# A four-layer graph network on one core: the opening's loads, transposes and query projection put in another order

## The reference, cut to what matters

```python
def _gate(h, q, Wg, bg, Wq, bq):        # q: 8 batches x 64 queries x 768
    h3 = h.reshape(B, N, F)
    hg = einsum('bnf,gf->bng', h3, Wg[:, :F])
    qg = einsum('blf,gf->blg', q, Wg[:, F:]) + bg
    attn = sigmoid(hg[:, :, None, :] + qg[:, None, :, :])
    qi = einsum('bnlf,blf->bnf', attn, q)
    alpha = sigmoid(einsum('bnf,gf->bng', h3, Wq[:, :F]) + einsum('bnf,gf->bng', qi, Wq[:, F:]) + bq)
    return alpha * tanh(qi) + (1.0 - alpha) * h3
def _rgcn(...):                          # sum over edges of type r, divided by their count at the node
    out = x @ W_root + bias
    for r in range(3): out = out + segment_sum(masked (x @ W_rel[r])[src], dst) / max(count, 1)
```

## Time and profile before

| | us |
|---|---|
| median of 3 runs | 302.65 (302.63 to 302.83) |
| profiled execution | 301.47 |
| its span | 299.7 |
| PE busy in the span | 270.3 (90%) |
| DVE, ACT, GpSimd busy | 150.9, 100.3, 97.3 |
| mean granted clock of TensorE | 0.988 |

### The profile page before, as it was taken

One profiled execution on the slowest core, in us unless ns is written; L12 is line 12 of the kernel. 1 busy time (PEld: TensorE's weight loads), 2 busy tenths in 40 slices (PEclk: granted clock), 3 DMA queues, 4 the chain that ended last, 5 costly groups with the idle time before them and its releaser, 6 DMA issues.

```text
span 299.7 us, 4436 instructions
## 1 busy us (share of the span) xinstructions
PE 270.3 (90%) x1839; PEld 127.6 (43%) x1839; DVE 150.9 (50%) x251; ACT 100.3 (33%) x166; POOL 97.3 (32%) x73
## 2 busy tenths in 40 slices
PE   0959999999989999989999899996998988997994
PEld 0855754445434652334434333332443443343441
DVE  4427502003798899742016898997243216223512
ACT  1323400004576996320005864655110014102100
POOL 7435000000389899400002899993000000000000
PEclk9979999999999999999999999999799999999999
DMA  5999993599001959100999910000099426000001
GB/s 189 287 326 373 401 403 155 168 405 374 3 1 33 406 196 317 4 0 2 329 403 401 400 45 2 0 2 0 4 365 403 175 68 249 3 0 0 2 0 26
DMA packets 20997, 51.85 MB, mean 173 GB/s; under 512 B 4073, under 2 KB 4329, under 8 KB 20978
## 3 DMA queue, kind: packets, MB, share of 16 engines
q1 hardware_dynamic: 20978, 51.58, 47.6%
HBM read 51.39 MB, written 0.20 MB: 172 GB/s over the span
## 4 chain that ended last, share of the span: by engine, by line
PE 59%; issue 19%; DVE 8%; DMA 5%; POOL 4%; ACT 3%; SPq 1%; DVEq 0%; POOLq 0%
PE ps L847 18%; PE ps L923 9%; PE ps L1015 5%; PE ps L1115 5%; DMA qn<-in_L_gnn_query_embs 5%; PE ps L987 4%; POOL prod L462 4%; PE ps L821 4%; PE ps L899 2%; DVE pre L714 2%; DVE prod L721 2%; PE ps L960 1%; PE ps L1181 1%; PE ps L885 1%; PE ps L937 1%
## 5 line engine op out<-in xcount | busy, mean ns | idle before, releaser
L462 POOL TENSOR_TENSOR prod<-pre,qn 128x768 f32<-128x768 f32 x39 | 81.8, 2126 | 96.4 <-ACT pre L534 94.4
L714 DVE TENSOR_TENSOR pre<-ps,qg 128x768 f32<-128x768 f32 x57 | 52.9, 951 | 8.8 <-PE ps L987 5.4
L534 ACT ACTIVATE pre<-pre 128x768 f32<-128x768 f32 x57 | 48.1, 849 | 21.5 <-DVE pre L714 21.0
L847 PE MATMUL ps<-W,prod 128*64 128x384 f32 x240 | 41.2, 503 | 0.0
L847 PE MATMUL ps<-W,nodeT 128*64 128x384 f32 x216 | 38.7, 492 | 0.0
L1015 PE MATMUL ps<-prod,rsel 128*32 128x192 f32 x512 | 33.9, 338 | 1.6 <-POOL prod L462 1.2
L987 PE MATMUL ps<-stack,bsel 96*128 96x384 bf16 x128 | 32.6, 330 | 2.5 <-DVE pre L714 2.2
L923 PE MATMUL ps<-W 128*128 128x384 f32 x96 | 33.8, 488 | 1.0 <-DVE W L335 0.9
L721 DVE TENSOR_TENSOR prod<-pre,qn 128x768 f32<-128x768 f32 x25 | 33.0, 1331 | 0.9 <-ACT pre L534 0.8
L335 ACT COPY W<-ps 128x384 f32<-128x384 f32 (+1 forms) x39 | 18.2, 495 | 37.8 <-PE ps L821 37.6
L847 PEld LDWEIGHTS ps<-W,prod 128*64 128x64 f32 x240 | 17.4, 141 | 22.1 <-issue 21.4
(11 more groups left out here) (168 smaller groups left out, 201.6 us busy)
## 6 DMA issues: line engine op xcount, KB each, us to landing
W<-in_L_gnn_W SPq DMA_DIRECT2D x9, 2304.0 KB, 10.7
W<-in_L_gnn_W_rel SPq DMA_DIRECT2D x6, 2304.0 KB, 15.0
W<-in_L_gnn_Wg SPq DMA_DIRECT2D x4, 1152.0 KB, 11.3
W<-in_L_gnn_W_root SPq DMA_DIRECT2D x2, 2304.0 KB, 11.7
W<-in_L_gnn_Wq SPq DMA_DIRECT2D x4, 1152.0 KB, 7.8
qn<-in_L_gnn_query_embs SPq DMA_DIRECT2D x2, 768.0 KB, 12.7
xa<-in_x SPq DMA_DIRECT2D x2, 96.0 KB, 15.4
out<-t SPq DMA_DIRECT2D x2, 96.0 KB, 2.2
```

The lines of the kernel that those rows point to most:

```text
L462: nc.gpsimd.tensor_tensor(prod[:, T % PRODS, :], pre[:, T % PRES, :], qn[:, t // NB, :], ALU.mult).then_inc(prod_p, 1)
L534: nc.scalar.activation(by_half(pre[:, T % PRES, :]), src, ACT.Sigmoid).then_inc(sig_ready, 1)
L714: nc.vector.tensor_tensor(by_half(pre[:, T % PRES, :]), ring(T), by_half(qg[:, t // NB, :]), ALU.add).then_inc(pre_ready, 1)
L847: ins = nc.tensor.matmul(ps[c * N:(c + 1) * N, bank, 0:HD], T[:, j, col0 + h * N:col0 + (h + 1) * N], w[:, k, c * HD:(c + 1) * HD], start= ...
```

## The change

- SP issues the first piece of `Wg_q`, query pair 0 (128 partitions in one transfer, with a semaphore of its own), the second piece, pairs 1 to 3, `Wg_h` and the relational weights. `rel1_2` still waits for the transposes of `Wg_q`, `root1` for those of `Wg_h`.
- ACT issues the three index transfers, computes one root of a column of the identity, and issues x and the nine biases, before its first copy.
- PE starts with 22 transposes of the identity, whose result nobody reads. Then come six groups of `Wg_q`'s first piece, two query groups (pair 0, three blocks each instead of four), half of unit 0 (three of its six products), six groups of the second piece, the other half of unit 0, half of unit 1, pair 1's groups, the counts, half of unit 1, unit 2, half of unit 3, the block matrices' transposes, half of unit 3, pairs 2 and 3, the 12 groups of `Wg_h`, `mix`, unit 4.
- DVE copies its groups up to query pair 0 ahead of the edge tables, the rest of `Wg_q` behind them, then does the counts, the degree chain, unit 0's copy, pair 1's copy and the block matrices. The mask (`maskb`) moves behind the copies of `Wg_h`.
- Query groups fill 384 columns, as the weights' do; counts, mix and block matrices get other PSUM banks.

The number of transposed blocks and of products is the same but for the 22. The diff, without most unchanged lines:

```diff
         ADDEND = 5
+        COUNTS, ADJ = 3, 0
+        WARM = 22
...
         x_loaded = sem("x_loaded")
-        q_loaded = sem("q_loaded")
+        q_loaded = [sem(f"q_{p}_loaded") for p in range(NP)]
+        M_ready = sem("M_ready")
...
-        G_Q = GROUPS
-        NQG = KC
-        G_H = G_Q + NQG
+        G_Q0 = KC
+        G_C1 = G_Q0 + 2
+        G_Q1 = G_C1 + KC
+        G_H = G_Q1 + 2 * (NP - 1)
...
         def mix_bank(layer, j):
-            return j + (5 if layer == 0 else 0)
+            return j + (1 if layer == 0 else 0)
...
-            if g < G_Q:
-                return WgT_q[:, g % KC, (g // KC) * HD:(g // KC + 1) * HD], HD
+            if g < G_Q0:
+                return WgT_q[:, g, 0:HD]
+            if G_C1 <= g < G_Q1:
+                return WgT_q[:, g - G_C1, HD:D]
             if g < G_H:
-                return qT[:, g - G_Q, :], NP * P
+                p, i = (0, g - G_Q0) if g < G_C1 else (1 + (g - G_Q1) // 2, (g - G_Q1) % 2)
+                return qT[:, i * JC:(i + 1) * JC, p * P:(p + 1) * P]
...
                 k = g - G_H
-                return WgT_h[:, k % KC, (k // KC) * HD:(k // KC + 1) * HD], HD
+                return WgT_h[:, k % KC, (k // KC) * HD:(k // KC + 1) * HD]
...
             dst = WqT_h if g - G_QH < GROUPS else WqT_q
-            return dst[:, k % KC, (k // KC) * HD:(k // KC + 1) * HD], HD
+            return dst[:, k % KC, (k // KC) * HD:(k // KC + 1) * HD]
...
         def copy_group(eng, g, done):
-            dst, n = group_dst(g)
+            dst = group_dst(g)
             eng.wait_ge(turned, g + 1)
-            src = ps[:, group_bank(g), 0:n]
+            src = ps[:, group_bank(g), 0:HD]
+            if G_Q0 <= g < G_C1 or G_Q1 <= g < G_H:
+                src = src.rearrange("p (k l) -> p k l", k=JC)
...
-            for i, name in enumerate(("src", "dst", "edge_type_3")):
-                sp.dma_start(eidx[:, i, :], a[name].rearrange("(p c) -> p c", p=P)).then_inc(edges_loaded, 16)
             Wg, Wq = a["L0_gnn_Wg"], a["L0_gnn_Wq"]
-            load("Wg_q", Wg[:, D:2 * D])
-            for b in range(2):
-                sp.dma_start(qn[b * L:(b + 1) * L, :, :],
-                             a["L0_gnn_query_embs"].rearrange("(p b) l f -> b l p f", b=2)[b]).then_inc(q_loaded, 16)
-            for i, name in enumerate(BIASES):
-                sp.dma_start(bias[i:i + 1, :], a[name].rearrange("(o f) -> o f", o=1)).then_inc(bias_loaded, 16)
+            queries = a["L0_gnn_query_embs"].rearrange("b l f -> (b l) f")
+            def load_queries(p):
+                sp.dma_start(qn[:, p, :], queries[p * P:(p + 1) * P, :]).then_inc(q_loaded[p], 16)
+            def load_part(key, dram, c):
+                n = KC // PARTS[key]
+                sp.dma_start(W[SLOT[key]][:, c * n:(c + 1) * n, :],
+                             halves(dram)[:, c * n:(c + 1) * n, :]).then_inc(loaded[key][c], 16)
+            load_part("Wg_q", Wg[:, D:2 * D], 0)
+            load_queries(0)
+            load_part("Wg_q", Wg[:, D:2 * D], 1)
+            for p in range(1, NP):
+                load_queries(p)
             load("Wg_h", Wg[:, 0:D])
-            for h in range(2):
-                sp.dma_start(xa[h * N:(h + 1) * N, :], a["x"][:, h * HD:(h + 1) * HD]).then_inc(x_loaded, 16)
...
             load("rel1_1", a["L0_gnn_W_rel1"][1])
-            load("rel1_2", a["L0_gnn_W_rel1"][2], turned, GROUPS)
+            load("rel1_2", a["L0_gnn_W_rel1"][2], turned, G_Q1)
...
-            for g in range(G_H):
-                if group_on_act(g):
-                    copy_group(act, g, turned_out_s)
+            for i, name in enumerate(("src", "dst", "edge_type_3")):
+                act.dma_start(eidx[:, i, :], a[name].rearrange("(p c) -> p c", p=P)).then_inc(edges_loaded, 16)
+            act.wait_ge(ident_ready, 1)
+            nc.scalar.activation(small[:, 42:43], ident[:, 0:1], ACT.Sqrt)
+            for h in range(2):
+                act.dma_start(xa[h * N:(h + 1) * N, :], a["x"][:, h * HD:(h + 1) * HD]).then_inc(x_loaded, 16)
+            for i, name in enumerate(BIASES):
+                act.dma_start(bias[i:i + 1, :], a[name].rearrange("(o f) -> o f", o=1)).then_inc(bias_loaded, 16)
+            def copy_groups(first, end):
+                for g in range(first, end):
+                    if group_on_act(g):
+                        copy_group(act, g, turned_out_s)
+            def unit_copy(u):
+                act.wait_ge(qg_done, u + 1)
+                nc.scalar.copy(qg[:, u // 2, (u % 2) * HD:(u % 2 + 1) * HD], ps[:, unit_bank(u), 0:HD]).then_inc(qg_out_s, 1)
+            copy_groups(0, G_Q1 + 2)
...
             act.wait_ge(sqrt_deg, 1)
-            nc.scalar.activation(small[:, 42:43], small[:, 9:10], ACT.Sigmoid)
...
+            nc.scalar.activation(small[:, 43:44], small[:, 9:10], ACT.Sigmoid)
             unit_copy(1)
-            for g in range(G_H, G_QH):
-                if group_on_act(g):
-                    copy_group(act, g, turned_out_s)
-            for u in range(3, SPLIT_UNIT, 2):
-                unit_copy(u)
+            copy_groups(G_Q1 + 2, G_H)
+            unit_copy(3)
+            copy_groups(G_H, G_QH)
...
+            def copy_groups(first, end):
+                for g in range(first, end):
+                    if not group_on_act(g):
+                        copy_group(dve, g, turned_out_v)
+            def unit_copy(u):
+                dve.wait_ge(qg_done, u + 1)
+                nc.vector.tensor_copy(qg[:, u // 2, 0:HD], ps[:, unit_bank(u), 0:HD]).then_inc(qg_out_v, 1)
+            copy_groups(0, G_C1)
...
                                         ALU.is_equal).then_inc(hot_ready, 1)
...
+            copy_groups(G_C1, G_Q1)
             dve.wait_ge(counts_done, 1)
-            link(nc.vector.tensor_copy(M[:, :], ps[:, 0, 0:R * N]))
-            copy_groups(range(G_H))
-            link(nc.vector.tensor_scalar(maskb[:, :], M[:, :], 0.0, NEG, ALU.is_equal, ALU.mult))
+            nc.vector.tensor_copy(M[:, :], ps[:, COUNTS, 0:R * N]).then_inc(M_ready, 1)
+            dve.wait_ge(M_ready, 1)
...
             link(nc.vector.reciprocal(small[:, 10:10 + R], small[:, 0:R]))
+            unit_copy(0)
+            copy_groups(G_Q1, G_Q1 + 2)
...
             nc.vector.tensor_scalar(blockd[:, R, :], blockd[:, R, :], small[:, 13:14], None, ALU.mult).then_inc(blocks_ready, 1)
...
-            unit_copy(0)
-            copy_groups(range(G_H, G_QH))
+            unit_copy(2)
             dve.wait_ge(adj_turned, 1)
-            nc.vector.tensor_copy(adjT[:, 0:R, :], ps[:, TRA, 0:R * P].rearrange("p (r n) -> p r n", r=R)).then_inc(adj_ready, 1)
-            nc.vector.tensor_scalar(gcnT[:, :], ps[:, TRA, R * P:(R + 1) * P], small[:, 13:14], None, ALU.mult).then_inc(adj_ready, 1)
-            for u in range(2, SPLIT_UNIT - 1, 2):
-                unit_copy(u)
+            nc.vector.tensor_copy(adjT[:, 0:R, :], ps[:, ADJ, 0:R * P].rearrange("p (r n) -> p r n", r=R)).then_inc(adj_ready, 1)
+            nc.vector.tensor_scalar(gcnT[:, :], ps[:, ADJ, R * P:(R + 1) * P], small[:, 13:14], None, ALU.mult).then_inc(adj_ready, 1)
+            copy_groups(G_Q1 + 2, G_QH)
+            link(nc.vector.tensor_scalar(maskb[:, :], M[:, :], 0.0, NEG, ALU.is_equal, ALU.mult))
...
-            pe.wait_ge(hot_ready, 3)
-            for c in range(EC):
-                ins = nc.tensor.matmul(ps[:, 0, 0:R * N], hot_dst[:, c, :], hot_src[:, c, :],
-                                       start=(c == 0), stop=(c == EC - 1))
-            ins.then_inc(counts_done, 1)
             pe.wait_ge(ident_ready, 1)
-            for k in range(GROUPS):
+            for _ in range(WARM):
+                nc.tensor.transpose(ps[:, TRB, 0:P], ident[:, :], ident[:, :])
+            def turn_queries(g, p):
+                pe.wait_ge(q_loaded[p], 16)
+                for i in range(2):
+                    wait_group_out(pe, g + i - 4)
+                    turn_blocks(g + i, [qn[:, p, k * P:(k + 1) * P] for k in range(i * JC, (i + 1) * JC)])
+            for k in range(KC):
                 turn_weight(0, "Wg_q", k)
-            pe.wait_ge(q_loaded, 32)
-            for k in range(NQG):
-                wait_group_out(pe, G_Q + k - 4)
-                turn_blocks(G_Q + k, [qn[:, p, k * P:(k + 1) * P] for p in range(NP)])
+            turn_queries(G_Q0, 0)
...
-            for u in range(SPLIT_UNIT):
-                if u == 0:
-                    wait_groups_out(pe, G_H)
-                if u == 2:
-                    for k in range(GROUPS):
-                        turn_weight(G_H, "Wg_h", k)
-                    wait_groups_out(pe, G_QH)
-                    pe.wait_ge(blocks_ready, 1)
-                    for r in range(R + 1):
-                        ins = nc.tensor.transpose(ps[:, TRA, r * P:(r + 1) * P], blockd[:, r, :], ident[:, :])
-                    ins.then_inc(adj_turned, 1)
-                if u == SPLIT_UNIT - 1:
-                    pe.wait_ge(x_loaded, 32)
```

(62 more changed lines are left out.)

3 lines of the change are left out of this document (removed).

## The result

| | before | after |
|---|---|---|
| median of 4 runs beside each other | 302.74 us (302.63 to 303.86) | 294.48 us (293.36 to 295.42) |
| profiled execution, its span | 301.47, 299.7 | 293.36, 291.6 |
| first relational product, in the chain | 50.89 | 42.90 |
| from there to the end of the span | 248.8 | 248.7 |

The ratio is 0.9718 [0.9669, 0.9766]: 8.3 us faster, where 5.6 were forecast. It is the first rival that happened (294.6 us). Between the two profiled executions 8.11 us are gained, and 7.99 of them stand in the opening.

What follows compares the result with a forecast made beforehand. Bound in the opening by TensorE and the late query transfers, up to the first relational product. Losses of 9.6 us become 4.3, start 0.3 earlier: gain 5.6, profiled 295.9, plus 1.2 to the median, 297.1 us; range 293.6 to 299.8.

Steps and rivals of the forecast that it cites:

- the first rival: Opening: GpSimd's bias operations do not collide with DVE's edge tables; gain 8.0, 294.6 us; chance 0.26.
- The main step: Opening: biases land around 9.5 to 10, so GpSimd's operations meet DVE's edge tables at 10.95; adds 2.4 us.
- the port: Opening: DVE's edge tables take turns with GpSimd's bias operations; 2.4 us added, PE stands 3.3 us at group 13.
- Two of the signs named beforehand: GpSimd's first bias operation after 14 would mean rival 1; first relational product before 43.5 would mean the forecast is wrong.
- rival 1: Opening: biases land later or the tables win, so no collision; PE stands 0.9; gain 8.0, 294.6 us; chance 0.26.
- rival 4: Opening: ACT's issues stay dear, ending at 9.7 instead of 7.4; gain 3.3, 299.4 us; chance 0.06.
- the sum's second form: Opening, cross-check: PE's work 34.2 us at fast pace; losses 9.6 before, 4.3 now, start 0.3 earlier; gain 5.6.
- The queries' rate: Opening: four query transfers over 128 partitions move at 396 GB/s; at 203 the sum would not hang on it.
- Rival 2: Opening: PE's stand at group 13 also lowers the clock, priced 1.2 to 1.9; gain 4.4, 298.3 us; chance 0.24.
- rival 3: Opening: the clock falls after each of several waits, 1.9 us each; four falls give 304.6 us; chance 0.05.
- The warm-up: Opening: 22 transposes from 1.5 us take 3.8, end before the weights, cost nothing; weights at fast pace; upper bound 1.1.
- 1.9 us either way: Behind the opening: the clock's fall at 210.4 us can vanish, or one like it appear at the first gate layer's end.

Runs made afterwards that it cites:

- tables_first_sp: The changed kernel with DVE's edge tables ahead of all its copies and the three index transfers back at the head of SP's list: 295.67 us, ratio 0.9828.
- tables_first: The changed kernel with DVE building the edge tables ahead of all its copies: 297.93 us, ratio 0.9885.
- no_warm: The changed kernel without its 22 warm-up transposes of the identity: 297.43 us, ratio 0.9801.
- q4_alone: The kernel before, with only its queries moved in four transfers of 128 partitions instead of two of 64: 295.23 us, ratio 0.9781.
- no_warm_late_split: The changed kernel without the 22 warm-up transposes and with GpSimd's bias splitting held back until the counts are done: 296.95 us, ratio 0.9859.
- transfers_alone: The kernel before with four query transfers and with ACT issuing indices, x and biases, the compute order as before: 299.41 us, ratio 0.9903.
- g15_early: The changed kernel with DVE's copy of group 15 ahead of its wait for the counts: 292.07 us, ratio 0.9629.
- after_again: The changed kernel, unaltered, timed once more beside the kernel before: 294.31 us, ratio 0.9706.
- g15_late_split: The changed kernel with group 15's copy ahead of the counts and GpSimd's bias splitting held back until the counts are done: 293.08 us, ratio 0.9696.
- bias_first: The changed kernel with the nine bias transfers ahead of x and of the first root on ACT: 293.75 us, ratio 0.9684.
- gate_warm: The changed kernel with more idle matmuls on PE at the end of both gate layers: 292.65 us, ratio 0.9651.
- both: The changed kernel with g15_early's and gate_warm's edits together: 293.00 us, ratio 0.9659.

## Why the prediction was right or wrong

**The main step was wrong.** Its words were "the index arrays … were in use two microseconds later … so I have the biases land around 9.5 to 10, and GpSimd's operations on them fall at 10.95, right on the edge tables". The index transfers of the earlier trace rows were the first on an empty machine (their first use, a cast at 3.29, came 1.6 us after the last issue). The biases are issued between 4.0 and 7.3 us, when SP has issued 3.9 MB (`Wg_q` and the queries) and adds the 2.4 MB of `Wg_h`, and the windows from 3 us on show a DMA share of 1.00 and above: they landed 6.4 us after the last issue, at 13.7. For the index arrays it is shown that their place does it: in use at 4.13 from the head of SP's list in tables_first_sp, at 8.95 from ACT in tables_first. That it is the backlog and not ACT's queue is shown by x: its two transfers, on ACT's queue in both, landed in 2.4 and 3.5 us when they were issued at 1.5 and 2.1, ahead of or with SP's first weights (tables_first_sp), and in 7.7 behind them (the change). For the biases it is argued from these. The rows of before had such a case too: the biases, issued by 7.5 behind weights and queries, were in use at 19.76. So the term "the port" is 0 instead of 2.4, and group 13 stands 0.32 instead of 3.3. Two of the signs named beforehand say so: GpSimd's first bias operation (L446 before, L460 now) starts at 13.78 instead of 11, and the relational product starts before 43.5. The time lies in the range only because that was drawn to take in rival 1. The price itself was right, 2.07 in no_warm for 2.4. What was wrong is whether it falls due. The transfers interleave, as the Trainium skill says on page "DMA: Bandwidth & Descriptors", section "Issuing engines are not separate DMA queues"; I read it as "they don't wait for SP's backlog", and the measured 4.1 to 7.1 us of the index arrays show that they do lose most of their time beside it.

**The other steps of the opening.** First weight at 6.80 for 6.5; ACT's first copy at 7.47 for 7.4, so the nine biases and the cheap x issues (0.83 each) were sized right, and rival 4 is out; half of unit 0 at 9.97 for 9.5, the start's 0.3 and ACT's 0.24 in it; the wait for group 15 0.69 for 0.7; the counts 0.82 for 0.8; the block matrices hidden behind unit 2, as said; Wg_h ending at 36.2 for 38.6, mix and unit 4 as long as forecast. Unit 4 ends at 42.62 for 45.0. By the sum's second form, 42.62 - 6.80 - 34.2 leaves 1.6 us lost (group 13 0.32, group 15 0.69, ACT 0.24, the rest at the weights' first transposes) where I had 4.3. The 2.7 less, minus 0.3 of start, is the 2.4.

**The queries' rate** was a choice (396 or 203 GB/s) on which the sum was said not to hang; it was 396. For the change that holds, for the kernel before it does not: q4_alone has 4.3 of the 8.0 us.

**Rival 2**, that a stand costs the clock, did not come because there was no stand; no_warm, tables_first and no_warm_late_split show it behind stands of 2.69, 4.46 and 2.13, tables_first_sp behind 2.49. It is no rule that a stand decides alone: q4_alone's 1.62 was followed by the full clock, and waits of 1.28 and 1.45 us later in the kernel by either. Waits of 0.3 to 0.95 were followed by the full pace in every profile, as was said against rival 3.

**The warm-up** was costed at nothing for its own time, and that is right, by little: it took 4.96 us instead of 3.8 and ended 0.3 before the weights. The 0.173 us per transpose (6.24/36) behind the 3.8 and behind the 0.52 per group was a mean over both paces; the slow one is 0.225. Its worth was not priced as a part of the sum: I took the fast pace "from the start" with an upper bound of 1.1 us, and in no_warm the six groups took 1.8 more. Without it the cost is 2.0 us up to group 13 alone, and by delaying DVE it also brings on the collision: 5.9 us of the opening in all.

**Behind the opening** the stretch was 248.7 for 248.8, and the fall at 210.4 neither vanished nor doubled in the profiled execution. "1.9 us either way" was somewhat too large for this place, 5.07 against 4.09 for the 24 products, and too small as a bound: the fall in the attention layer, which other executions have, costs 2.2 to 3.7. The stretch without any fall is 247.2 us, in transfers_alone (50.75 to the span's end at 298.0) and in g15_early (41.38 to 288.6).

**From the span to the median** I added 1.2 us for the profiled execution of before being on the low side. That one had 301.47 against a median of 302.74, the new one 293.36 against 294.48: it held, by the draw of two runs at a clock of .992 and two at .982. At nearly the same clock, the fastest of before (298.43 at .999, beside the last four runs) and of the change (291.79 at .997, after_again) are 6.6 us apart; of the 8.0 gained in the opening, 1.5 were the fall of the clock in it.

## What to carry to other kernels

A transfer's landing time is read from a row that had the same backlog beside it, never from the first transfers of a program; and before pricing a collision of two engines, find out how many tenths of a microsecond decide whether it takes place. Where a first stage is short of data, put the work that needs the first large transfer ahead of what waits for small ones, and look at the shape of the transfers: four over 128 partitions for two over 64 were half of this gain. To tell changes of less than 1% apart, read each run's mean granted clock beside its time, and the stretch in the trace that the change touches.

## What the runs showed of the hardware that was not expected

- The queries in two transfers into 64 partitions moved at 203 to 234 GB/s (11 to 17 us) at a DMA share of 0.99 to 1.08, the same bytes in four into 128 partitions at 396 to 409 (q4_alone, 11 to 16 us).
- Three index arrays of 12 KB in all took 1.6 to 1.9 us each to land on the idle machine and 4.1 to 7.1 from ACT beside SP's first 1.6 MB; x took 2.4 to 3.5 ahead of most of it and 7.7 behind it; the nine biases took 6.4.
- When operations of GpSimd and DVE fall together, one can wait for a whole operation of the other: 0.16 us became 1.60 (no_warm_late_split, L647), two tables of 1.29 together became 3.36, and GpSimd's 0.81 became 1.36.
- Executions of one kernel fall into steps by how much of them runs at 1.2 GHz: mean clocks of 0.999, 0.992, 0.986, 0.982 and 0.976, from 290.8 us at 0.999 to 296.4 at 0.976 in g15_late_split. The profiles at .999 (g15_early, transfers_alone) have no such stretch ahead of the last microseconds, the changed kernel's at .992 has one, behind the gate layer, and those at .976 (bias_first, g15_late_split) have that one and a longer one in the attention layer. The moments differ between kernels whose work there is the same.
- A fall began behind waits of PE of 1.28 us (before, 209.62) and 1.45 us (gate_warm, 241.44); g15_early has a wait of 1.29 and one of 1.45 in the same places and no fall behind either.
- Which code would keep the clock up over the whole program is open. The medians of g15_early (292.07), gate_warm (292.65), both (293.00), g15_late_split (293.08) and bias_first (293.75) lie below the changed kernel's 294.3 to 294.5, but their intervals overlap its interval, and only g15_early's 1.2 us can also be pointed at in the opening. It is the best version measured: 292.07 us, 0.9629 of before.
